# Tree feed-forward of a two-layer decoder: logits, routes and first gathers of batch 0 placed inside the last column steps of the first attention run

## The reference, cut to what matters

```
x = x + L0_attn(layernorm(x))                 # random-feature attention
x = x + L0_xattn(layernorm(x), ctx, mask)     # softmax, 16 heads of 8 channels
x = x + L0_ffn(layernorm(x))                  # the tree feed-forward
x = x + L1_attn(layernorm(x)); x = x + L1_xattn(layernorm(x), ctx); x = x + L1_ffn(x)
```

```
def _fff(x, nw, nb, w1, b1, w2, b2, act):
    node = 0
    for _ in range(8):
        logit = sum(x * nw[node]) + nb[node]
        node = 2 * node + 1 + (logit > 0)
    leaf = node - 255
    h = act(sum(x * w1[leaf]) + b1[leaf])      # 16 hidden values of a token
    return h @ w2[leaf] + b2[leaf]
xn = (x - mean) / sqrt(std(ddof=1) + 1e-5)     # of the layernormed x
y = xn + softmax(q @ k.T / sqrt(128)) @ v      # q, k, v = _fff(xn, ..., relu)
out = y + _fff(y, f..., gelu)
```

## Time and profile before

| | us |
|---|---|
| median of 3 runs (785.63 to 791.99) | 787.99 |
| the profiled execution | 788.61 |
| its span in the profile | 786.9 |
| PE busy in the span | 662.3 (84%) |
| DVE busy | 603.8 (77%) |
| ACT busy | 442.1 (56%) |
| POOL busy | 321.1 (41%) |

### The profile page before, as it was taken

The page is one execution under the profiler, slowest core; times in us unless marked ns, Lnnn a source line. Parts: engine busy times, 40 slices in busy tenths (PEclk is TensorE's granted clock), DMA queues, the critical chain, the costliest instruction groups (busy, mean ns, idle before and its releaser), DMA issues. The chain is left out here.

```text
span 786.9 us, 14564 instructions
## 1 busy us (share of the span) xinstructions
PE 662.3 (84%) x4849; PEld 506.1 (64%) x4849; DVE 603.8 (77%) x2434; ACT 442.1 (56%) x1064; POOL 321.1 (41%) x315
## 2 busy tenths in 40 slices
PE   4869979686949989998879699999879688888998
PEld 2547525344437877877758467665445578888997
DVE  6894677763398999996869877787636689999984
ACT  1333106455046987988987155566655665555562
POOL 3150422911133423333125332222012698888983
PEclk9985559898568999999999999999999899999999
DMA  8000121100197999899634122221000000000000
GB/s 249 4 0 3 29 58 45 41 3 1 45 409 297 381 362 402 327 405 416 232 153 161 48 51 52 59 54 44 5 1 1 1 1 5 4 5 5 4 5 8
DMA packets 38931, 86.07 MB, mean 109 GB/s; under 512 B 3993, under 2 KB 30146, under 8 KB 30664
## 3 DMA queue, kind: packets, MB, share of 16 engines
q0 software_dynamic: 9216, 69.47, 22.5%
q1 hardware_dynamic: 29640, 15.67, 7.5%
HBM read 74.43 MB, written 0.52 MB: 95 GB/s over the span
## 5 line engine op out<-in xcount | busy, mean ns | idle before, releaser
L833 ACT ACTIVATE arena<-arena,hact 128x128 f32<-128x128 f32 x512 | 155.4, 388 | 1.0
L611 POOL TENSOR_TENSOR arena<-arena 128x1024 f32<-128x1024 f32 x64 | 121.1, 1911 | 22.0 <-DVE arena L1296 16.4
L716 ACT ACTIVATE arena<-psum 128x512 f32<-128x512 f32 (+1 forms) x192 | 101.1, 561 | 48.5 <-PE psum L1454 48.0
L1153 DVE CUSTOM_DVE_ANT_0 arena<-arena,fx 128x128 f32<-128x128 f32 x384 | 106.1, 347 | 7.8 <-DMA arena<-tab_q,leaf_no 6.9
L879 ACT ACTIVATE psum<-arena,tneg 128x1024 f32<-128x1024 f32 x64 | 71.5, 1118 | 61.8 <-DVE arena L1296 29.1
L1821 PE MATMUL psum<-arena 128*128 128x128 f32 x688 | 91.1, 294 | 16.4 <-DVE arena L1296 10.0
L967 DVE TENSOR_REDUCE rowmax<-psum 128x2 f32<-128x512 f32 x128 | 81.3, 687 | 23.7 <-PE psum L1436 21.9
L1821 PEld LDWEIGHTS psum<-arena 128*128 128x128 f32 x688 | 87.6, 209 | 18.4 <-DVE arena L1296 11.1
L1713 PE MATMUL psum<-identf,arena 128*128 128x128 f32 x544 | 78.1, 298 | 15.8 <-ACT arena L833 14.8
L1713 PEld LDWEIGHTS psum<-identf,arena 128*128 128x128 f32 x544 | 70.2, 206 | 23.6 <-ACT arena L833 17.0
L1436 PE MATMUL psum<-arena 128*128 128x256 bf16 (+1 forms) x384 | 73.2, 282 | 9.5 <-DVE rowmax L967 8.0
(11 more groups left out here) (233 smaller groups left out, 1198.8 us busy)
## 6 DMA issues: line engine op xcount, KB each, us to landing
arena<-parts SPq DMA_DIRECT2D x144, 64.0 KB
w_sb<-attn_w SPq DMA_DIRECT2D x1, 768.0 KB, 8.0
x<-x_in SPq DMA_DIRECT2D x1, 512.0 KB, 4.2
fx<-ctx_in SPq DMA_DIRECT2D x1, 512.0 KB, 5.2
picked<-mask_in SPq DMA_DIRECT2D x1, 512.0 KB, 6.3
wq_sb<-peer_wq SPq DMA_DIRECT2D x1, 512.0 KB, 7.2
down_sb<-table_down SPq DMA_DIRECT2D x1, 512.0 KB, 8.0
up_sb<-table_up SPq DMA_DIRECT2D x1, 512.0 KB, 8.6
```

The source lines that it names most:

```text
L611: nc.gpsimd.tensor_tensor(grid[k % 3].rearrange("p (i j) -> p i j", i=PK), sim[:, t, h, :].unsqueeze(2).to_broadcast([P, PK, PK]), sim[:, ...
L716: nc.scalar.activation(probs[k % (2 * HG)][:, 0:w], bank(2 + k % 2, 0, w), ACT.Exp, scale=float(D) ** -0.5).then_inc(probs_ready, 1)
L833: a = nc.scalar.activation(w, w, ACT.Copy, scale=hact[i % 2][:, l:l + 1])
L1153: i = nc.vector.tensor_tensor_reduce(w, w, src, 1.0, r[:, LW * E + l:LW * E + l + 1], ALU.mult, ALU.add, hid[g % 4][:, l:l + 1])
```

## The change

**The last step of the first run (n = 7).** DVE does `ffn_norm(0, 0, 4)` right behind `max_parts(7)`, in step 6, ahead of `onorm(6)`. PE does `turn_fx(0)` behind the columns of head 0 of step 7, and the six logits of batch 0 one at a time behind heads 2, 3, 4, 5, 9 and 10 (`some_logits`), in banks 0 and 1, which the score rows no longer need. ACT copies the transposed input behind head 1, into the buffer `xn_t0`. DVE descends in two parts: trees q and k (4 of the 6 logits) at head 6, tree v at head 11 (`walk_some`).

**After the run.** PE turns and makes the logits of batch 1 there (they stood ahead of leaf 0), among them `turn_out(7)` and `tail_a(7)`; `tail_b(7)` comes behind them. On DVE `onorm(7)` moves behind `hidden(0)`, `resid(7)` and the route of batch 1 behind `hidden(2)`. On ACT the copy for `tail_b(7)` moves behind leaf 0.

**Gathers and memory.** The ring buffers change places. Gather 0 may start while the run is going on; the w1 gather of step 1 also waits for the last column product (`cols_ps`), the w2 gather of step 1 for the last value product (`pv_ps`). Before the last clear POOL also waits for the last `fh_ready`.

The core of the diff:

```diff
-        leaf1 = [arena[:, i:i + ROW1] for i in (2 * ROW2, 5 * ROW2 + 2 * ROW1, 3 * ROW2 + ROW1)]
+        leaf1 = [arena[:, i:i + ROW1] for i in (5 * ROW2 + 2 * ROW1, 2 * ROW2, 3 * ROW2 + ROW1)]
-        leaf2 = [arena[:, i:i + ROW2] for i in (ROW2, 4 * ROW2 + 2 * ROW1, 3 * ROW2 + 2 * ROW1, 2 * ROW2 + ROW1, 0)]
+        leaf2 = [arena[:, i:i + ROW2] for i in (0, 4 * ROW2 + 2 * ROW1, 3 * ROW2 + 2 * ROW1, 2 * ROW2 + ROW1, ROW2)]
-        fx_t = arena3[:, 0:256]
+        fx_t = [xn_t[0][:, :]] + [arena3[:, 0:256]] * (B - 1)
+        FX_BANK = [0, 3, 4, 4]
...
-        VECTOR_AT = {("route", 1): 1, ("norm", 1): 4, ("route", 2): 10, ("weigh", 0): 10, ("attend", 0): 11,
+        VECTOR_AT = {("out", 2 * B - 1): 1, ("resid", 2 * B - 1): 3, ("route", 1): 3, ("norm", 1): 4, ("route", 2): 10, ("weigh", 0): 10, ("attend", 0): 11,
...
@@ POOL, gathers @@
-                        pool.wait_ge(idx_ready, b + 1)
+                        pool.wait_ge(idx_ready, b + 2 if b else 1 + f // 2)
+                    if g == 1:
+                        pool.wait_ge(cols_ps, B * H)
...
+                    if g == 1:
+                        pool.wait_ge(pv_ps, B + B * H)
...
+                pool.wait_ge(fh_ready, len(ORDER))
@@ ACT, run @@
+                        if n == 2 * B - 1 and h == 1:
+                            evac_fx(0)
...
                 if first == B:
-                    evac_fx(0)
+                    evac_fx(1)
@@ ACT, ffn (SCALAR_AT has ("out", 2 * B - 1): 1) @@
+                    elif what == "out":
+                        evac_ot(i)
@@ DVE, run @@
-                if first == B:
-                    ffn_norm(0, 0, 2 * SUB)
-                else:
+                        if first == B and (n, h) == (last - 1, 11):
+                            ffn_norm(0, 0, 2 * SUB)
+                        if first == B and n == last:
+                            if h == 6:
+                                walk_some(0, 4, 1)
+                            elif h == 11:
+                                walk_some(4, 6, 2)
+                if first > B:
                     peer_norm(0, 0, 2 * SUB)
-                onorm(last)
-                if first == B:
-                    walk_of(0)
-                resid(last)
+                    onorm(last)
+                    resid(last)
...
+            def walk_some(a, z, part):
+                dve.wait_ge(lg_ps, part)
+                route(z - a, 0, leaf_no[0][:, a:z], (dec_ready, 1, part), (idx_ready, 1, part))
@@ PE, run @@
+                        if first == B and n == last:
+                            if h == 0:
+                                turn_fx(0)
+                            elif h in (2, 3, 4, 5):
+                                some_logits(h // 2 - 1, h % 2)
+                            elif h in (9, 10):
+                                some_logits(2, (h - 1) % 2)
                 values(last, HG - 1)
                 if first == B:
-                    turn_fx(0)
+                    turn_fx(1)
+                    turn_out(last)
+                    tree_logits(1, 0)
+                    tail_a(last)
+                    tree_logits(1, 1)
+                    tree_logits(1, 2)
+                    tail_b(last)
...
             def turn_fx(b):
                 pe.wait_ge(fx_ready, b // 2 + 1)
+                if b == 0:
+                    pe.wait_ge(rows_max, B * H)
...
+            def some_logits(f, s):
+                pe.wait_ge(fxt_ready, 1)
...
+                if f == 2 and s == 0:
+                    pe.wait_ge(dec_ready, 1)
+                i = logits(s, f, fx_t[0], bank(f % 2, s * S, s * S + S))
+                if f >= 1 and s == SUB - 1:
+                    i.then_inc(lg_ps, 1)
```

More of the change, by code:

```diff
@@ L333, in decoder_program @@
         ORDER += [(b, s, 3) for b in range(B) for s in range(SUB)]
-        TENSOR_AT = {("turn", 1): 0, ("turn", 2): 4, ("score", 0): 7, ("mix", 0): 10, ("turn_f", 0): 11,
+        TENSOR_AT = {("turn", 2): 4, ("score", 0): 7, ("mix", 0): 10, ("turn_f", 0): 11,
                      ("turn", 3): 12, ("score", 1): 14, ("mix", 1): 16, ("turn_f", 1): 18, ("score", 2): 20,
@@ L339, in decoder_program @@
                      ("next", NEXT[0]): 28, ("next", NEXT[1]): 32}
[L340 removed]
+        SCALAR_AT = {("out", 2 * B - 1): 1, ("turn", 2): 4, ("weigh", 0): 10, ("mix", 0): 10, ("turn_f", 0): 11,
                      ("turn", 3): 12, ("weigh", 1): 16, ("mix", 1): 16, ("turn_f", 1): 18, ("weigh", 2): 22,
@@ L783, in run @@
                     evac_sims(0)
-                evac_ot(last)
-                if first > B:
+                    evac_ot(last)
                     evac_sims(1)
@@ L789, in evac_fx @@
                 act.wait_ge(fxt_ps, b + 1)
-                copy(fx_t[:, :], bank(4 if b else 3, 0, S), fxt_ready)
+                copy(fx_t[b], bank(FX_BANK[b], 0, S), fxt_ready)
             def evac_px(i):
@@ L1184, in ffn @@
                         norm(i)
+                    elif what == "out":
+                        onorm(i)
+                    elif what == "resid":
+                        resid(i)
                     elif what == "leaf":
@@ L1651, in run @@
                             max_turn(n + 1)
+                        if first == B and n == last:
[5 more added lines that the diff above has]
+                                some_logits(2, (h - 1) % 2)
                 values(last, HG - 1)
                 if first == B:
-                    turn_fx(0)
+                    turn_fx(1)
[5 more added lines that the diff above has]
+                    tail_b(last)
                 else:
                     turn_px(0)
-                turn_out(last)
-                if first == B:
-                    tree_logits(0)
-                else:
+                    turn_out(last)
                     sims(0)
-                tail_a(last)
-                if first > B:
+                    tail_a(last)
                     sims(1)
-                tail_b(last)
+                    tail_b(last)
             def logits(s, f, src, o):
@@ L1679, in turn_fx, with tree_logits @@
                 for s in range(SUB):
-                    j = (4 if b else 3) * BANK + s * P
+                    j = FX_BANK[b] * BANK + s * P
                     i = nc.tensor.transpose(psum[:, j:j + P], fx[:, SUB * b + s, :], identf[:, :])
                 i.then_inc(fxt_ps, 1)
-            def tree_logits(b):
-                if b == 0:
+            def some_logits(f, s):
+                pe.wait_ge(fxt_ready, 1)
+                if f == 0 and s == 0:
                     pe.wait_ge(in_tab, 32)
                     pe.wait_ge(nbias_ready, 1)
-                else:
-                    pe.wait_ge(dec_ready, b)
-                pe.wait_ge(fxt_ready, b + 1)
-                for f in range(3):
-                    for s in range(SUB):
-                        i = logits(s, f, fx_t, bank(f, s * S, s * S + S))
-                i.then_inc(lg_ps, 1)
+                if f == 2 and s == 0:
[3 more added lines that the diff above has]
+                    i.then_inc(lg_ps, 1)
+            def tree_logits(b, f):
+                if f == 0:
+                    pe.wait_ge(dec_ready, b + 1)
+                    pe.wait_ge(fxt_ready, b + 1)
+                for s in range(SUB):
+                    i = logits(s, f, fx_t[b], bank(f, s * S, s * S + S))
+                if f == 2:
+                    i.then_inc(lg_ps, 1)
             def ffn():
@@ L1720, in ffn @@
                         turn_fx(b)
-                        tree_logits(b)
+                        for f in range(3):
+                            tree_logits(b, f)
                     elif what == "next":
```

5 lines of the change are left out of this document (2 added, 3 removed).

## The result

The changed kernel takes 779.97 us (median of 19 runs, 774.96 to 789.05), the kernel before in the same comparison 788.54 (19 runs, 785.63 to 793.60). The ratio is 0.9878, with a 95% interval of 0.9858 to 0.9898: 9.6 us faster, between 8.0 and 11.2. This ratio leaves out one execution of the changed kernel that fell in a slower state (789.05), and it is not the quotient of the two medians, which are 8.6 us apart. The prediction was 14.6 us and 774.0. Two further comparisons gave 0.9877 [0.9843, 0.9911] and 0.9857 [0.9826, 0.9888].

The account below looks back on a forecast made before the run. Up to leaf 4 DVE's chain was taken to bound the kernel, from there ACT. Last column at 199.8 plus 40.4 puts leaf 4 at 240.2 instead of 254.85: 788.6 - 14.6 = 774.0 us, range 768 to 784.

Parts of the forecast that it names:

- The stall: Step 7, PE behind head 0's columns: it stands from 176.7 until fx is there at 181.45.
- the half clock behind it: Step 7, PE after its wait for fx: 3.4 us of work at 1.2 GHz, costing 1.7 us.
- Rival B: Step 7: PE's clock stays at 1.2 GHz throughout, last column at 209, gain 5.5, time 783; chance 0.12.
- Rival C: Behind leaf 4: a fixed pace, first of all the gather stream, absorbs the gain; time 788; chance 0.10.
- Rival D: Leaves on PE: late queue at half clock, 7.0 us each against ACT's 5.1; 8 us slower, 796; chance 0.06.
- hidden(1) starts at C + 6.7: Behind the last column product: gather 1 waits for it and takes 6.7 us from leaf numbers to hidden values.
- C: End of the last column product of the first run: 188.85 before, forecast 199.8, ends 197 and 209.
- From C to leaf 4: Last column product to ACT's leaf 4: sum 40.4 us, leaf 4 at 240.2 instead of 254.85.
- has long landed: Ahead of hidden(0), behind the last column: gather 0 is already there, so hidden(0) lies under gather 1.
- from leaf 4 on the engines go in step behind ACT ... nothing behind leaf 4 is altered: Behind leaf 4: ACT sets the pace, so the change gives what ACT gets leaf 4 earlier, 14.6 us.
- every later mark of the kernel earlier by the same 15 us: Sign in the changed profile: ACT's leaf 4 at 240, and the 15 us carries to all later marks.
- slack that might run out: PE's late queue behind the run, leaves 0 to 4: costs nothing unless over 3 us later.

Follow-up runs that it names:

- e2: Changed kernel with 36 products of zeros on PE ahead of the turn of batch 0, during its stall; 776.90 us, ratio 0.9836.
- e1: Changed kernel with the turn of batch 0 moved from head 0 to head 6 and its logits and descents later; 777.63 us, ratio 0.9871.
- e3b: Second comparison of the same kernel as e3, zero products in PE's two gaps of the leaf stage; 777.23 us, ratio 0.9837.
- e4: Kernel before with only the descent of batch 1 moved, ahead of leaf 3 and not leaf 1; 791.70 us, ratio 1.0018.
- e6: e5 with onorm(7) and its copy back ahead of leaf 0; 774.70 us, ratio 0.9821.
- e7: e6 with zero products at the two places of e3, 46 and 14 of them; 775.84 us, ratio 0.9799.
- r2_after: Changed kernel run a third time, unaltered, for the scatter of profiles; 779.41 us, ratio 0.9857.
- e5: e1 with tree q's logits and descent first, trees k and v behind heads 11 to 14; 775.96 us, ratio 0.9842.
- r_after: Changed kernel run a second time, unaltered, for the scatter of profiles; 778.12 us, ratio 0.9877.
- e3: Changed kernel with 20 products of zeros ahead of leaf 3 and 18 ahead of the turn of batch 2 on PE; 777.65 us, ratio 0.9860.
- r_before: Kernel before run again, unaltered, for a second profile of it; 788.73 us (one run).

## Why the prediction was right, and where it was wrong

**What was right.** Forecast and measured, in us behind the anchor: last column 28.5 and 27.3 to 28.4; leaf 4 68.9 and 69.9 to 70.9. fx was scaled 10.2 us behind the anchor (183.56 + 1.11 - 174.45), as forecast (181.45 - 171.28). The stall was 4.67 us where 4.75 was summed; the half clock behind it lasted about 3.3 us of work where 3.4 was taken, and its price by e2 was 1.5 to 2.6 us where 1.7 stood. From the turn to the last column the sum had 17.6 us, 15.9 of it without the clock; it took 16.4 to 17.4, and 15.1 in e2, where the clock stayed up. Rival B, the half clock to the end of the run, is refuted by the row of 188 to 190 us. Rival C, a fixed pace behind leaf 4, is refuted by e1 and e3b: with leaf 4 some 14 us earlier they take 529.5 and 529.3 us from leaf 4 to the last add, and the kernel before 529.8 and 530.5. Rival D would have needed a last column at 209. (The 34 records of the earlier trace rows are one leaf step, as the prediction counts them, not two as their heading has it; and the 23.6 us of the earlier trace rows hold the turns and logits of batches 0 and 1.) The Trainium skill, "TensorE: Matmul & The Clock Gate", section "Part 1: The HAM clock gate", has it that activity releases the throttled clock; in this step the trace agrees (0.50 to 1.00 by 188), in the logits of the kernel before it does not (0.50 over 22.5 busy us), and e4 shows the same logits of batch 0 released.

**A term that was mis-sized: "hidden(1) starts at C + 6.7".** From C to leaf 4 the sum had 40.4 us; it is 42.5 in all three profiles of the changed kernel (69.9 - 27.3, and so on). hidden(1) started at C + 8.9 (210.64 against 201.78), 2.2 us late, and that is the difference. Two things are in it. POOL issued gather 1 at C + 0.8, not at C. And its use was 8.08 us behind its issue, not the 6.35 of gather 0 before (211.62 to 217.97; the 6.7 counts from the leaf numbers), since the second transfer of gather 0 had been issued only 3.35 us ahead of it (199.21) and was still in the stream: 417 GB/s in the row of 202 to 204 us. In the other five profiles with this order it was used 7.54 to 8.12 us behind its issue. I had written of gather 0 that it "has long landed"; DVE waited 2.48 us for it. Its time of issue was right (195 with the anchor at 171.28 is 23.7 behind it; it came at 23.2), and from there 6.5 us to its use and the second transfer behind it reach past C. e6 shows the cure: gather 0 at 18.4, gather 1 used after 6.15 us. Of the wait at hidden(1), about 1 us was forecast and 1.04 came. The Trainium skill, "DMA: Bandwidth & Descriptors", section "Anatomy of one DMA — SWDGE (gpsimd) path", has a fit by which the estimate for such a gather is 4.4 us; the trace does not agree: where DVE waited for a gather with nothing ahead of it, its use came 5.98 (e7) to 6.61 us (e1) behind its issue.

**The step that failed** is "from leaf 4 on the engines go in step behind ACT ... nothing behind leaf 4 is altered", and with it "every later mark of the kernel earlier by the same 15 us". Of 13.1 us at leaf 4, 4.9 do not arrive at the end. Two places are seen in the traces.

The first is the logits of batch 2. In both profiles of the kernel before, PE came to their turn from a queue of late leaf work and did not stand. I counted that lateness only as slack that might run out; in truth it kept PE busy. Now PE is ahead and stands for fx. In five profiles (changed, r2_after, e2, e5, e6) it stood 1.63 to 2.21 us and the clock then fell; leaf 6 comes 12.8 to 14.2 us behind leaf 4 there, and 10.2 in the eight others. So it costs 2.6 to 4.1 us when it happens (leaf 4 to 18 takes 88.7 to 90.8 us against 86.2 to 87.2). In the eight others PE stood 1.50 us (r_after), 1.41 (e4), 0.65 (e1), 0.23 to 0.67 (the three with filler ahead of this turn) and not at all (the two of the kernel before).

The second is in the second run. The windows between two residual additions, first of the changed kernel:

```profile
557.20:572.20 15.00, 12.73 (x115) 6.27 (x114) 2.24 (x10) 10.13 (x19) 0.00 (x0) 0.89 0.01 3
...
572.30:588.60 16.30, 11.98 (x84) 6.92 (x82) 7.21 (x36) 6.34 (x11) 2.01 (x2) 0.79 0.00 2
```

and of the kernel before the same two steps:

```profile
565.40:579.40 14.00, 11.32 (x116) 6.02 (x117) 2.28 (x11) 10.13 (x19) 0.00 (x0) 1.00 0.01 3
579.40:594.70 15.30, 10.90 (x84) 6.07 (x82) 7.32 (x37) 6.35 (x11) 2.01 (x2) 0.89 0.01 2
```

The same instructions take 1.1 and 1.2 us longer (additions at 557.17, 572.23 and 588.66 against 565.42, 579.38 and 594.65), and the clock is lower by a tenth. These are 2.3 of the 2.7 us that this profile loses behind leaf 18. The first of the two steps takes 13.96 to 13.99 us in eight profiles and 14.91 to 15.06 in the other five, which are all of the changed order (changed, r2_after, e3, e5, e7). The code there is the same in all. The five have one stretch at 0.50 of 3.4 us in this step, 6.2 to 6.5 us behind the addition, and the eight have none. In the changed kernel it is in this window:

```profile
563.00:567.00 4.00, 3.44 (x22) 1.15 (x22) 0.00 (x0) 2.41 (x5) 0.00 (x0) 0.57 0.00 0
```

PE had stood 1.29 and 0.47 us just ahead of it; in the kernel before it stood 1.27 and 0.47 us there, and the clock stayed up. The second step is longer in the profile of the changed kernel alone.

By these marks the two places make 4.8, 5.0 and 0 us in the three profiles of the changed kernel, 3.3 of the 4.9 on the mean. The rest lies in other places.

**What stays open:** why the clock falls more often in the changed order so far behind the change. It may be the other time at which each stretch begins, and it may be chance: only three profiles have the old order, and three of the ten others (r_after, e1, e3b) show no loss at either place. r_after loses 1.8 to 2.2 us behind leaf 18 all the same; it has stretches at 1.2 GHz of 3.4 us at 383.3 and at 427.7 us, where the kernel before has none. No run separates these. Nor do the times show that the two places are what parts 14.6 from 9.6 us: the filler at the first place gave no gain clear of the intervals, and the account rests on marks of three profiles against two.

## What to carry to other kernels

A gain on a chain need not carry to the end in full: work that arrives earlier at an engine that was late turns its queue into idle time, and on TensorE the clock of what follows fell behind such idle time in five of the seven profiles without filler there (1.63 to 2.21 us of it). When work is moved under a wait, follow the first transfers through to their use, and see what is ahead of each in its stream: here gather 1 took 8.1 us behind a late gather 0, and 6.15 behind an early one. And compare marks from an event ahead of the change, in several profiles, since one pair showed 5.8 us where the times show 9.6.

## What the runs showed of the hardware that was not expected

The same program with nearly the same waits gets different clocks. After idle times of 1.65 and 0.57 us the logits took 1.48 us each from the fall at 242.6 on in the changed kernel's profile, after 1.50 and 0.56 us 0.84 each in r_after. In step 7, behind waits of 1.28 to 1.29 and 0.47 us, the clock fell in e1 and e5 and not in e6, which is the same program as e5 up to there. The logits behind the first run stayed at 1.2 GHz through the 23.6 us of the earlier trace rows in the kernel before, and as long in r_before; in e4, whose program is the same up to there, PE was at full clock again after 2.8 us of work.

Not every half-clock stretch costs: the profile of the kernel before has six of them of 3.4 us between 646 and 753 us, that of the changed kernel one, at 744, and the stretch from the last addition of the second run to the last add takes 190.0 and 190.2 us.
